# Q, K and V projections: token blocks outside, weight blocks inside, with all weights kept in SBUF

## The reference, cut to what matters

```python
def _layernorm(x, axis=-1, eps=1e-5):
    m = jnp.mean(x, axis=axis, keepdims=True)
    v = jnp.var(x, axis=axis, keepdims=True)
    return (x - m) / jnp.sqrt(v + eps)
...
    def _L0_attn_ref(x, W_qkv, b_qkv, W_out, b_out):
...
        qkv = x @ W_qkv.T + b_qkv
        q, k, v = jnp.split(qkv, 3, axis=-1)
        q, k, v = (to_heads(q), to_heads(k), to_heads(v))
        scores = jnp.einsum('bnqd,bnkd->bnqk', q, k) * scale
        scores = jnp.where(causal, -jnp.inf, scores)
        attn = jax.nn.softmax(scores, axis=-1)
        out = jnp.einsum('bnqk,bnkd->bnqd', attn, v)
...
    x = x + _L0_attn_ref(_layernorm(x, axis=-1), L0_attn_W_qkv, L0_attn_b_qkv, L0_attn_W_out, L0_attn_b_out)
    x = x + _L0_ffn_ref(_layernorm(x, axis=-1), L0_ffn_gate_w, L0_ffn_Wg, L0_ffn_Wu, L0_ffn_Wd, L0_ffn_sWg, L0_ffn_sWu, L0_ffn_sWd)
```

## Time and profile before

| | us |
|---|---|
| median of the 2 runs shown | 6852.73 (6765.78 and 6939.67) |
| the profiled execution, its own time | 6610.32 |
| its span, first to last instruction, slowest core (core 3) | 6608.8 |
| spans of the other cores | 6543.7 to 6589.9 |
| TensorE busy, all of the span | 4790.3 (72%) |
| VectorE, ScalarE, GpSimd busy | 2326.3, 1153.5, 813.6 |

### The profile page before, as it was taken

One profiled execution on the slowest core, in us unless ns is written; L12 is line 12 of the kernel. 1 busy time (PEld: TensorE's weight loads), 2 busy tenths in 40 slices (PEclk: granted clock), 3 DMA queues, 4 the chain that ended last, 5 costly groups with the idle time before them and its releaser, 6 DMA issues.

```text
span 6608.8 us, 79844 instructions; the slowest of 8 cores (6543.7 to 6608.8 us)
## 1 busy us (share of the span) xinstructions
PE 4790.3 (72%) x23616; PEld 2194.8 (33%) x23616; DVE 2326.3 (35%) x5032; ACT 1153.5 (17%) x1908; POOL 813.6 (12%) x1541
## 2 busy tenths in 40 slices
PE   1942799997676667666666668678787818888874
PEld 1421344443332333323333323333333313333332
DVE  5035100001554555545555424422232333322214
ACT  0110111111334333343333400000000000000000
POOL 1520133331000000000000000111212011212120
PEclk9965899998666666766667689799999959999997
DMA  3543233333000000000000054342524262334233
GB/s 110 71 108 108 56 58 58 57 58 80 17 17 17 33 17 17 17 17 33 17 11 11 1 153 166 64 71 39 77 39 77 39 165 39 56 59 68 47 64 108
DMA packets 254427, 383.07 MB, mean 58 GB/s; under 512 B 128833, under 2 KB 211009, under 8 KB 231489
## 3 DMA queue, kind: packets, MB, share of 16 engines
q0 software_dynamic: 221328, 176.32, 18.0%
q1 hardware_dynamic: 32690, 201.64, 8.5%
HBM read 453.41 MB, written 83.89 MB: 81 GB/s over the span
## 4 chain that ended last, share of the span: by engine, by line
PE 57%; DVE 17%; issue 8%; DMA 7%; ACT 6%; POOL 4%; DVEq 1%; ACTq 0%; SPq 0%; POOLq 0%
PE psA L357 7%; PE psB L357 7%; DVE cmax L450 6%; ACT pt L459 5%; PE psT L221 4%; PE psD L765 4%; PE psE L759 3%; PE psA L789 3%; POOL slot L672 3%; PE psC L759 3%; PE psA L444 3%; PE psB L765 3%; PE psC L528 2%; PE psB L444 2%; DMA slot<-wu 2%
## 5 line engine op out<-in xcount | busy, mean ns | idle before, releaser
L444 PE MATMUL psA<-qf,kf 128*128 128x512 bf16 (+3 forms) x1280 | 559.0, 470 | 180.1 <-DVE cmax L450 77.3
L444 PE MATMUL psB<-qf,kf 128*128 128x512 bf16 (+3 forms) x1280 | 529.5, 446 | 149.4 <-DVE cmax L450 64.6
L459 ACT ACTIVATE pt<-psA,biasap 128x512 bf16<-128x512 f32 (+3 forms) x640 | 402.3, 629 | 1282.4 <-DVE psA L456 538.3
L357 PE MATMUL psA<-xnf,wkb 128*128 128x512 bf16 x2048 | 454.9, 380 | 0.0
L357 PE MATMUL psB<-xnf,wkb 128*128 128x512 bf16 x2048 | 452.5, 379 | 0.0
L450 DVE TENSOR_REDUCE cmax<-psA 128x1 f32<-128x512 f32 (+1 forms) x640 | 407.6, 637 | 51.9 <-DVE cmax L450 9.6
L459 ACT ACTIVATE pt<-psB,biasap 128x512 bf16<-128x512 f32 (+3 forms) x640 | 395.5, 618 | 115.0 <-DVE psB L456 63.3
L450 DVE TENSOR_REDUCE cmax<-psB 128x1 f32<-128x512 f32 (+2 forms) x640 | 373.4, 583 | 58.2 <-DVE cmax L450 10.0
L349 POOL DMA_DIRECT2D wkb<-wqkv_t x512 | 271.3, 604 | 905.4 <-PE psB L357 869.5
L221 PE MATMUL psT<-ident_bf,xn 128*128 128x128 bf16 x768 | 97.0, 306 | 386.3 <-DVE xn L247 340.6
L789 PE MATMUL psA<-slot,tdf 128*128 128x512 bf16 x1408 | 337.8, 379 | 0.0
(11 more groups left out here) (124 smaller groups left out, 5564.2 us busy)
## 6 DMA issues: line engine op xcount, KB each, us to landing
xt<-x_own SPq DMA_DIRECT2D x32, 1024.0 KB, 5.9
xt<-x_seq SPq DMA_DIRECT2D x32, 1024.0 KB, 5.3
slot<-wg POOLq DMA_DIRECT2D x256, 128.0 KB, 5.7
slot<-wu POOLq DMA_DIRECT2D x256, 128.0 KB, 9.5
slot<-wd POOLq DMA_DIRECT2D x64, 512.0 KB, 16.9
wkb<-wqkv_t POOLq DMA_DIRECT2D x512, 32.0 KB, 2.6
kf_s<-kvb SPq DMA_DIRECT2D x16, 1024.0 KB, 4.5
vf_s<-kvb SPq DMA_DIRECT2D x16, 1024.0 KB, 4.6
```

The lines of the kernel that those rows point to most:

```text
L357: (lambda E, i=i, o=o, n=n, k=k, pj=pj: E.matmul(ps4[pj], wkb_34[k][:, i * 128:(i + 1) * 128], xnf[:, i * S + n * 512: i * S + (n + 1) * 512],
L444: em.emit("t", lambda E, kt=kt, g=g, hb=hb, jmin=jmin, N=N, stb=stb: E.matmul(stb[:, 0:N], kf_sb[hb][:, kt * 128:(kt + 1) * 128], qf_sb[hb ...
L459: em.emit("s", lambda E, kt=kt, N=N, stb=stb, gb=gb: E.activation(pt_sb[gb][:, kt * 512: kt * 512 + N], stb[:, 0:N], AF.Exp, bias=bias_ap[ ...
```

## The change

In Q, all 16 weight blocks get buffers of their own (wq8, 64 KB of each partition) and are fetched ahead of the loop; the loop over token blocks `n` is outside and that over `o` inside. Each result of 128x512 goes through one of four small buffers (qst) and is stored at once, 64 stores of 128 KB in place of 16 of 512 KB.

In K and V the same: wkv holds all 32 blocks (128 KB of each partition). To make room, xnf_r holds only 8 tiles of normalised x, as a ring. Eight tiles are normalised first. Then for each of 8 token blocks `n` (a "pass" below) all 32 blocks `o` are computed, 32 x 16 matmuls, with a store of 128 KB for each; and after passes 0 to 5 the next four tiles are normalised into the ring places that the pass has just read (the `ln_tile34` loop at the end). They are read two passes later. The numbers of instructions on TensorE, VectorE and ScalarE don't change; stores become 256 in place of 32.

```diff
+        qst = [sb12(f"qst{j}", [128, 512], BF16) for j in range(4)]
+        r_qst = [Res() for _ in range(4)]
+        wq8 = [sb12(f"wq8_{j}", [128, 2048], BF16) for j in range(16)]
+        r_wq8 = [Res() for _ in range(16)]
         for o in range(16):
-            k = o % 2
             em.dma("g", [
-                (lambda E, o=o, i=i, k=k: E.dma_start(
-                    out=wqb_12[k][:, i * 128:(i + 1) * 128], in_=wqkv_t[o, i]))
+                (lambda E, o=o, i=i: E.dma_start(
+                    out=wq8[o][:, i * 128:(i + 1) * 128], in_=wqkv_t[o, i]))
                 for i in range(IC)
-            ], writes=[r_wqb[k]])
-            for n in range(nOQ):
-                pj = (o * nOQ + n) % 4
-                rd = [r_wqb[k]] + [r_xnow[tt] for tt in range(n * 4, n * 4 + 4)]
+            ], writes=[r_wq8[o]])
+        for n in range(nOQ):
+            rdt = [r_xnow[tt] for tt in range(n * 4, n * 4 + 4)]
+            for o in range(16):
+                pj = (n * 16 + o) % 4
                 em.emit_group("t", [
-                    (lambda E, i=i, o=o, n=n, k=k, pj=pj: E.matmul(
-                        ps4[pj], wqb_12[k][:, i * 128:(i + 1) * 128],
+                    (lambda E, i=i, o=o, n=n, pj=pj: E.matmul(
+                        ps4[pj], wq8[o][:, i * 128:(i + 1) * 128],
                         xnow[:, i * OWN + n * 512: i * OWN + (n + 1) * 512],
                         start=(i == 0), stop=(i == IC - 1)))
                     for i in range(IC)
-                ], reads=rd, writes=[r_ps4[pj]])
-                em.emit("s", lambda E, o=o, n=n, k=k, pj=pj: E.activation(
-                    qbuf_12[k][:, n * 512:(n + 1) * 512], ps4[pj], AF.Identity,
+                ], reads=[r_wq8[o]] + rdt, writes=[r_ps4[pj]])
+                sj = (n * 16 + o) % 4
+                em.emit("s", lambda E, o=o, pj=pj, sj=sj: E.activation(
+                    qst[sj][:], ps4[pj], AF.Identity,
                     bias=sbq_sb[:, o:o + 1], scale=SCL),
-                    reads=[r_ps4[pj], r_sbq], writes=[r_qbuf[k]])
-            em.dma("y", lambda E, o=o, k=k: E.dma_start(out=qf_s[o], in_=qbuf_12[k][:]),
-                   reads=[r_qbuf[k]], writes=[r_qfs[o]])
+                    reads=[r_ps4[pj], r_sbq], writes=[r_qst[sj]])
+                em.dma("y", lambda E, o=o, n=n, sj=sj: E.dma_start(
+                    out=qf_s[o][:, n * 512:(n + 1) * 512], in_=qst[sj][:]),
+                    reads=[r_qst[sj]], writes=[r_qfs[o]])
 
...
-        xnf = sb34("xnf", [128, IC * S], BF16)
+        xnf_r = sb34("xnf_r", [128, IC * 1024], BF16)
...
-        for t in range(nTT):
+        r_xnfr = [Res() for _ in range(8)]
+
+        def ln_tile34(t):
             k = t % 2
             em.dma("y", lambda E, t=t, k=k: E.dma_start(out=xt_34[k][:],
                                                         in_=x_seq[t * 128:(t + 1) * 128, :]),
                    writes=[r_xt34[k]])
             emit_ln(xt_34[k], r_xt34[k], xn_34[k], r_xn34[k], sm_34[k], r_sm34[k],
                     bnb_34[k], r_bnb34[k])
-            xfv = xnf[:].rearrange("p (i s) -> p i s", i=IC)
+            xfv = xnf_r[:].rearrange("p (i s) -> p i s", i=IC)
+            ts = t % 8
             emit_tpose([xn_34[k][:, i * 128:(i + 1) * 128] for i in range(IC)], None,
-                       [r_xn34[k]], [r_xnf[t]],
-                       batch_dsts=[xfv[:, 0:8, t * 128:(t + 1) * 128],
-                                   xfv[:, 8:16, t * 128:(t + 1) * 128]])
+                       [r_xn34[k]], [r_xnfr[ts]],
+                       batch_dsts=[xfv[:, 0:8, ts * 128:(ts + 1) * 128],
+                                   xfv[:, 8:16, ts * 128:(ts + 1) * 128]])
+
+        for t in range(8):
+            ln_tile34(t)
 
         nSQ = S // 512
+        kst = [sb34(f"kst{j}", [128, 512], BF16) for j in range(4)]
+        r_kst = [Res() for _ in range(4)]
+        wkv = [sb34(f"wkv{o}", [128, 2048], BF16) for o in range(32)]
+        r_wkv = [Res() for _ in range(32)]
         for o in range(16, 48):
-            k = o % 2
             em.dma("g", [
-                (lambda E, o=o, i=i, k=k: E.dma_start(
-                    out=wkb_34[k][:, i * 128:(i + 1) * 128], in_=wqkv_t[o, i]))
+                (lambda E, o=o, i=i: E.dma_start(
+                    out=wkv[o - 16][:, i * 128:(i + 1) * 128], in_=wqkv_t[o, i]))
                 for i in range(IC)
-            ], writes=[r_wkb[k]])
-            for n in range(nSQ):
-                pj = (o * nSQ + n) % 4
-                rd = [r_wkb[k]] + [r_xnf[tt] for tt in range(n * 4, n * 4 + 4)]
+            ], writes=[r_wkv[o - 16]])
+        for n in range(nSQ):
+            rdt = [r_xnfr[tt % 8] for tt in range(n * 4, n * 4 + 4)]
+            c0 = (n % 2) * 512
+            for oo in range(32):
+                o = 16 + oo
+                pj = (n * 32 + oo) % 4
                 em.emit_group("t", [
-                    (lambda E, i=i, o=o, n=n, k=k, pj=pj: E.matmul(
-                        ps4[pj], wkb_34[k][:, i * 128:(i + 1) * 128],
-                        xnf[:, i * S + n * 512: i * S + (n + 1) * 512],
+                    (lambda E, i=i, oo=oo, c0=c0, pj=pj: E.matmul(
+                        ps4[pj], wkv[oo][:, i * 128:(i + 1) * 128],
+                        xnf_r[:, i * 1024 + c0: i * 1024 + c0 + 512],
                         start=(i == 0), stop=(i == IC - 1)))
                     for i in range(IC)
-                ], reads=rd, writes=[r_ps4[pj]])
-                em.emit("s", lambda E, o=o, n=n, k=k, pj=pj: E.activation(
-                    kvb_34[k][:, n * 512:(n + 1) * 512], ps4[pj], AF.Identity,
+                ], reads=[r_wkv[oo]] + rdt, writes=[r_ps4[pj]])
+                sj = (n * 32 + oo) % 4
+                em.emit("s", lambda E, o=o, pj=pj, sj=sj: E.activation(
+                    kst[sj][:], ps4[pj], AF.Identity,
                     bias=bqkv_sb[:, o:o + 1], scale=1.0),
-                    reads=[r_ps4[pj], r_bqkv], writes=[r_kvb[k]])
-            if o < 32:
-                em.dma("y", lambda E, o=o, k=k: E.dma_start(out=kf_s[o - 16], in_=kvb_34[k][:]),
-                       reads=[r_kvb[k]], writes=[r_kfs[o - 16]])
-            else:
-                em.dma("y", lambda E, o=o, k=k: E.dma_start(out=vf_s[o - 32], in_=kvb_34[k][:]),
-                       reads=[r_kvb[k]], writes=[r_vfs[o - 32]])
+                    reads=[r_ps4[pj], r_bqkv], writes=[r_kst[sj]])
+                if o < 32:
+                    em.dma("y", lambda E, o=o, n=n, sj=sj: E.dma_start(
+                        out=kf_s[o - 16][:, n * 512:(n + 1) * 512], in_=kst[sj][:]),
+                        reads=[r_kst[sj]], writes=[r_kfs[o - 16]])
+                else:
+                    em.dma("y", lambda E, o=o, n=n, sj=sj: E.dma_start(
+                        out=vf_s[o - 32][:, n * 512:(n + 1) * 512], in_=kst[sj][:]),
+                        reads=[r_kst[sj]], writes=[r_vfs[o - 32]])
+            for t in range(8 + 4 * n, min(8 + 4 * n + 4, nTT)):
+                ln_tile34(t)
 
         em.fence()
         p34.close()
```

More of the change, by code:

```diff
@@ L257, in build_nc @@
         bnb_12 = [sb12(f"bnb12_{k}", [128, 24], F32) for k in range(2)]
-        wqb_12 = [sb12(f"wqb12_{k}", [128, 2048], BF16) for k in range(2)]
-        qbuf_12 = [sb12(f"qbuf12_{k}", [128, OWN], BF16) for k in range(2)]
         r_xt = [Res(), Res()]
@@ L265, in build_nc @@
         r_xnow = [Res() for _ in range(nQT)]
-        r_wqb = [Res(), Res()]
-        r_qbuf = [Res(), Res()]
         r_qfs = [Res() for _ in range(NH)]
@@ L320, in build_nc @@
         bnb_34 = [sb34(f"bnb34_{k}", [128, 24], F32) for k in range(2)]
-        wkb_34 = [sb34(f"wkb34_{k}", [128, 2048], BF16) for k in range(2)]
-        kvb_34 = [sb34(f"kvb34_{k}", [128, S], BF16) for k in range(2)]
         r_xt34 = [Res(), Res()]
@@ L327, in build_nc @@
         r_bnb34 = [Res(), Res()]
-        r_xnf = [Res() for _ in range(nTT)]
-        r_wkb = [Res(), Res()]
-        r_kvb = [Res(), Res()]
-        for t in range(nTT):
+        r_xnfr = [Res() for _ in range(8)]
+        def ln_tile34(t):
             k = t % 2
```

## The result

The changed kernel is slower by 2.2%: a ratio of 1.0218 to the kernel before (95% interval 1.0184 to 1.0253), median 7024.6 us over 12 runs against 6848.5 over 10 of the kernel before, where 7003 was predicted. The profiled execution has a span of 6733.8 us, 125 more than before. The executions of both kernels spread by several per cent, because in some of them the cores of a die show a lower granted clock; the ratio is taken without those, and two experiments are read on cores 4 to 7, whose mean clock was the usual 0.82.

A forecast was written before the change was run, and what follows sets the result against it. K/V was bound first by VectorE's LayerNorm, then by TensorE. 684 + 270 + 790 = 1744 us for the last K/V matmul, against 1592.5, less some 2, gave +150: 6852.7 + 150 = 7003 us, range 6800 to 7120.

The forecast's parts named there:

- Pass 0 ends: K/V's first pass, held by GpSimd's weight issues, ends at 684 us; bounds 664 and 727.
- the pauses: GpSimd's K/V weight issues: one in some 80 comes after 1.87 us of waiting, 11 us in all.
- The wait for weights: K/V pass 0: TensorE waits for weight blocks, ending at 684 us against 588 without the wait, +96 us.
- The gaps: After K/V passes 0 to 5, four tiles are normalised serially: six of 45 us, 270, +39 beyond tiles replaced.
- The passes: K/V: seven passes of 112.9 us each, 790 us together; lower bound 785.
- The clock starts: K/V: the first 32 matmuls after each gap run slow, 2.4 us more; +14 us for six.
- Cover: Q: weight issues out by about 144 us beside x_own's LayerNorm, before the first matmul at 165; nothing charged.
- rival C: K/V pass 0: DMA side can't carry the weights; pieces at 0.7 us each, total +226, 7079 us; chance 0.12.
- Attention: Attention, untouched by the change, stays 2180 us long as before.
- Rival D: Attention: clock granted 10% more often returns some 150 us, 6853 or below; chance 0.08.
- Rival B: K/V gaps: x loads in time, a gap 31.7 us, total +70, 6923 us, within 2%; chance 0.10.
- The range's upper end: K/V: first pass ending at 727 us, plus 296 for gaps and 790 for later passes, gives +221 us.

The follow-up runs named there:

- the first experiment: The changed kernel with the loads of a gap's first two x tiles emitted ahead of the pass's stores: attention starts at 1665.9 to 1672.0 us, against 1730.1 to 1735.8.

## Why the prediction was right, step by step

The landmark moved by 142.3 us where +150 was forecast; the last K/V matmul ends at 1736.7, where 1744 was forecast. By terms:

- **Pass 0 ends**: 684 forecast, 678.2 measured. The pace of the issues came out: 0.562 us while VectorE normalises (394.47 to 475), where 0.554 was taken, and 0.519 behind it, as taken. The step that was off is the pauses: I counted 11 us for six more pauses of 1.87 us inside the run, taken from a trace in which GpSimd had stood still before each group. There is one pause, the first. Against that stands the long last issue, so the issues end at 669.4 instead of 676. My reason for the 0.554, DMA engines close to full, was wrong: all of the surplus is the eight held issues, some 6 us. The Trainium skill (SBUF — State Buffer, Who interferes with whom) has VectorE shut GpSimd out for the whole instruction, and I had put that at 11 us for eight. The trace agrees that the issue due next waits for the instruction's end, but the distance of two issues grows by 0.76 us and not by 1.35: one issue still starts 0.18 us into the instruction, and only the next, due 0.52 later, is held. The 256 pieces of Q show the same: 0.565 us each over 144.72 us, with fourteen distances of 1.15 to 1.56 us.
- **The wait for weights** was +96 in the sum; TensorE spent 204.1 us on pass 0 and 112.0 on the mean of the others: 92. The experiments with two token blocks and with one DMA each took it away, by two different ways, 81 and 91 us at the landmark.
- **The gaps**: 270 forecast for six of 45; measured 46.0, 45.7, 45.5, 46.1, 46.0 and 45.1, 274, which is +43 beyond the tiles that they replace, where +39 was forecast. The chain was as forecast, load 5.9 us in the median. That part of it hangs on the order in SP is shown by the first experiment, that all of it was a matter of order by LayerNorm inside the passes.
- **The passes**: 790 forecast, 784 measured. The clock starts cost 1.1 to 2.4 us each, with 2.4 taken: the first 32 matmuls after a gap took 8.18 to 9.46 us against 7.07 for later ones. The sum also charges seven starts, where six passes stand behind a gap.
- **Cover**: Q's weights at no cost, right to within the scatter. The DMA engines were at 0.96 from 0 to 160 us, and the loads of x landed in 6.3 us in the median against 5.9. In the experiment with one DMA a block x landed in 11.3 us (median, 390 to 600 us): close to the 13.5 that they have, and not holding their own beside the weights, as I had supposed. There the engines' share was 1.29 from 400 to 470 us, so the 1.0 on which rival C leaned was not full.
- **Attention** did not change (0.67; output projection's first weights at 3944.6 against 3800.7, +143.9). Rival D is out. Rival B and rival C are out by rows shown above: a gap over 42 us, a pace under 0.6.
- **The range's upper end** doesn't come out of its own terms: pass 0 at 0.604 us an issue ends at 394.3 + 512 x 0.604 + 9.7 + 6.9 = 720, not 727, and 0.604 is the mean length of issues that overlap in the record; their time for one is 271.3/512 = 0.53.

Not all of the nearness is merit. The wait and the clock starts were put 4 us each too high and the gaps 4 too low. And the median of 7003 added to the profiled execution an excess of 242 us that nothing explained: it was 238 in the kernel before (6848.5 over 6610.3) and 289 in the changed one (7024.6 over 6735.3). That 7003 is only 22 us from 7024.6 is in part luck; what bears out the working is the ratio and the landmark.

What stays open is the 17 us that the profiled execution has less behind the landmark.

## What to carry to other kernels

When two loops are exchanged so that weights are kept, the first sweep must bring all the weights in the time of one sweep: compare the queue's time for a block (here 8.3 us, 16 issues of 0.519) with the engine's work on it (3.5 us), and give the first sweep more work for each block, or make the issues fewer and larger. Work that is put between two sweeps is serial unless each list that it passes through has it early: here the run that interleaved it in SP, ScalarE and TensorE took the gaps away, and moving two of the four loads in SP alone brought 11 of 46 us. A wait that is 1000 us long in the table of waits can be worth 11 us a time, and the place of the work in each engine's list, which was worth the other 35, is no line of that table.

## What the runs showed of the hardware that was not expected

- A DMA issue on GpSimd took 1.14 us for 2048 rows of 512 B and 0.53 for 128 rows: 16 times the rows for about twice the time.
- In a stream of such issues, 0.519 us apart, the one that fell due during VectorE's 1.35 us float32-to-bf16 instruction started 0.11 us after its end, a loss of 0.76 us a time in the last six of eight.
- 512 consecutive issues had one pause of 1.87 us, at the first; the same 512, issued in 32 groups with rests between them, had seven. The cause is not known.
- A DMA engines' share of 1 in the windows doesn't mean that they are full: with one large DMA a block it read 1.48, and a block came every 4.7 us, where it read 0.83 (480 to 660 us of the changed kernel) with a block every 8.3.
- With Q's matmuls nearly without a break on all eight cores (129 to 138 of 140 us), two cores of one die were granted 0.80 of the clock, neither full nor half, and their matmuls slowed nearly in proportion (8.57 against 7.07 us for 32), in an execution that was among the fastest of its kernel. In the kernel before, all eight cores had 1.00 on K and V for 860 us.
